# Seven pieces of an embedding table by plain loads and GpSimd adds, in a fused patch-embedding, attention and routed-expert kernel

## The chip, the cores and the metric

The kernel runs on one core of one Trainium2 chip. The metric is the device time of one execution in microseconds, given as the median of several runs. A program runs on five engines, each with its own instruction queue: TensorE (PE in the profile; its weight loads are PEld), VectorE (DVE), ScalarE (ACT), GpSimd (POOL) and SyncE (SP). They are ordered by semaphores alone. DMAs that SP and ACT issue are called hardware_dynamic in the profile, those that POOL issues software_dynamic.

## The reference

Eight images of 3x96x96 are cut into 36 patches each, projected to 192 features and joined with 128 text rows, so there are 8 batches of 164 rows. Then come one attention layer with 12 heads and one routed-expert layer with 16 experts. The part that matters here is one term of the attention: the mean row of a table of 50257x192 numbers.

```
xn = _layernorm(x, ln_w)
avg_wte = jnp.mean(wte, axis=0)                       # 50257 x 192 -> 192
Q = xn[:, None, :, :] * W_qk[None, :, None, :]
attn = jnp.einsum('bhse,bhte->bhst', Q, Q) / math.sqrt(eb)
attn = softmax(where(causal, attn, -inf))
Vv = xn[:, None, :, :] - avg_wte[None, None, None, :]
out = jnp.einsum('bhst,bhte->bhse', attn, Vv) * N_reg # N_reg = 1 / (1..164)
out = out.transpose(0, 2, 1, 3).reshape(xb, sb, H * eb) @ W_o.T
h = h + out
...
h = h + moe(_layernorm(h))   # rms norm, softmax router, 16 experts, 64 rows per expert and batch
```

## The kernel before

**Stages.** After the loads and the patch projection (to about 21 us) there is an attention loop over eight batches, b = 0 to 7 (to about 270 us), then the router and the placing of the rows into a DRAM buffer `xd` ("dispatched" in the profile) with one 112-row block per expert or more, and from about 310 us a loop over these blocks. The rows of `xd` that no token fills have to hold zeros and a marker. Seven DMAs write them from the tile `zeros` ("dispatched<-zeros"), and the scatters into `xd` wait for them on `zero_done`.

**The table.** The table is 38.6 MB and is summed while the attention runs. It is seen as 28 pieces of 128 x 2688 numbers (1344 KB each: 14 rows of the table per partition) and a small tail. The tile `wbuf` has two halves. SP loads pieces 0 and 1 into them (`wte_first`). POOL then issues 26 DMAs that add their piece to what the half holds (`add_wte`, L369 to L377; "wbuf<-in_wte"). The halves take turns, so that two such DMAs are under way, and `add_wte` first waits until the one before it into the same half has landed. Iteration b of POOL's loop issues four of them, k = 0 to 3. At the end DVE sums `wbuf` over its 28 rows (`wte_sum`, four instructions at L700), adds the tail and signals `acc_ready`. The mean is then projected by TensorE near 245 us. It is subtracted late and not in the loop.

**One iteration of attention.** The scores of a batch are made in five rounds: rounds 0 to 2 cover the first 128 rows, four heads each, into the banks `bS`; rounds 3 and 4 cover the last 36 rows. For each round TensorE writes the scores (`score`), DVE takes the row maximum (L663, L667), ACT the exponential with its row sum (L496, L501), DVE the factor `rn` (L673, L675), and POOL multiplies (`normalise`, L387: tile PA for rounds 0 to 2, PB for 3 and 4). TensorE transposes the result (L1062 and on), ACT and DVE split the transposed tile into a high and a low part (L509, L680), and TensorE multiplies it by the values. POOL also makes the left operand of the scores: `weigh` (L365) multiplies the transposed input `zT` by the weights of each head, into AwA (six instructions of 96 x 512 a batch) and AwB (two of 96 x 432).

**Order on POOL.** Iteration b of POOL does, in this order: rounds 3 and 4 of batch b; `add_wte` k = 0; four AwA of batch b + 1; k = 1; two AwA; round 0 of batch b + 1; k = 2; round 1; two AwB; k = 3; round 2. TensorE's first score round of batch b + 1 waits for the first two AwA, so it waits for what stands ahead of them on POOL.

**DVE between two batches.** DVE makes the low parts of the values (`value_low`, L690 and L692), the normalised input of the batch after (`z`, L655 and L657: from SBUF to SBUF), then the row maximum of round 2.

**SP's queue.** SP issues the loads, waits for `zero_ready`, issues the seven zero fills, then the load of `mat32` (tile `pay`), waits for `acc_ready` and loads the first expert weights into the tiles `wx`, which are free until then.

## Time and profile before

| what | value |
|---|---|
| median of 3 runs | 407.25 us (407.04 to 409.11) |
| the profiled execution: its own time | 410.09 us |
| the profiled execution: its span | 408.2 us |
| its granted TensorE clock, mean | 0.942 |
| TensorE busy | 349.9 us, 86% |
| VectorE busy | 196.3 us, 48% |
| GpSimd busy | 181.7 us, 45% |
| ScalarE busy | 119.5 us, 29% |
| moved by DMA | 74.28 MB, mean 182 GB/s |

Busy is the time in which instructions of an engine run. The share is that of the whole span. Times given as a point, such as "at 156.34", are microseconds from the start of the span. In a row of a timeline the first number is the start, the second the length, and what stands in brackets at the end is how long the engine sat idle before it and what released it.

### The profile page before, as it was taken

To read this page: it belongs to the slowest core of one execution; us is meant where nothing else is said; L and a number is where in the kernel's file an instruction comes from. 1 tells how busy PE (TensorE), PEld (TensorE's weight loads), DVE (VectorE), ACT (ScalarE), POOL (GpSimd) and SP (SyncE) were. 2 spreads that over 40 slices of the span, in tenths; PEclk is the share of its full clock that TensorE was granted. 3 is DMA by queue.
4 is the path that set the end of the run, shared out by engine and by line. 5 is a ranking of instruction groups with operands and counts; after the bars stand their busy time and mean duration, and the time that the engine had idled before them with its cause. 6 is when DMAs were issued, how large, how long until landed. Compare 5 with 4: busy or idle time off the path is not lost.

```text
span 408.2 us, 6960 instructions
## 1 busy us (share of the span) xinstructions
PE 349.9 (86%) x2371; PEld 314.5 (77%) x2371; DVE 196.3 (48%) x532; ACT 119.5 (29%) x411; POOL 181.7 (45%) x189
## 2 busy tenths in 40 slices
PE   7878889589789899898899999995684998999990
PEld 3456579578689789797899898895534998999990
DVE  0495865737536456355472575678660221222220
ACT  1115333332744456345543133333100011111110
POOL 3164573385576674857655131611377421111110
PEclk9989999699999999999999999998586898999996
DMA  6599999999999999999995008800133497899700
GB/s 218 193 372 265 233 251 247 256 217 209 200 173 209 212 209 210 205 210 205 207 209 119 0 2 247 217 0 2 53 117 82 137 295 198 267 287 285 240 14 9
DMA packets 20735, 74.28 MB, mean 182 GB/s; under 512 B 3180, under 2 KB 8813, under 8 KB 20202
## 3 DMA queue, kind: packets, MB, share of 16 engines
q0 software_dynamic: 8976, 38.83, 46.3%
q1 hardware_dynamic: 10826, 34.57, 27.4%
q10 hardware_dynamic: 912, 0.62, 0.6%
q8 instruction: 12, 0.20, 0.2%
q14 instruction: 9, 0.07, 0.1%
HBM read 66.12 MB, written 9.25 MB: 185 GB/s over the span
## 4 chain that ended last, share of the span: by engine, by line
DMA 43%; PE 34%; issue 8%; POOL 6%; DVE 3%; SPq 1%; ACT 1%; POOLq 1%; ACTq 1%; DVEq 0%
DMA wbuf<-in_wte 34%; PE bO L991 11%; PE bE L991 10%; PE bJ L991 6%; DMA AwA<-dispatched 6%; PE bS L991 4%; DMA hB<-in_txtB 3%; POOL AwA L365 2%; POOL dispatched L430 2%; POOL wbuf L376 1%; PE bT L1308 1%; POOL PB L387 1%; PE bT L1062 1%; DMA dispatched<-pay,posI 1%; DVE wsum L700 1%
## 5 line engine op out<-in xcount | busy, mean ns | idle before, releaser
L496 ACT ACTIVATE PA<-bS,negmax 128x128 f32<-128x128 f32 x96 | 33.9, 366 | 94.2 <-DVE negmax L663 94.2
L365 POOL TENSOR_TENSOR AwA<-zT,w 96x512 f32<-96x512 f32 x45 | 52.4, 1448 | 7.4 <-ACT zT L478 7.4
L991 PE MATMUL bJ<-wo_sb,oTA 128*128 128x192 f32 x288 | 51.5, 327 | 0.7 <-DVE H L706 0.7
L376 POOL DMA_DIRECT2D wbuf<-in_wte x26 | 32.1, 1255 | 44.3 <-DMA wbuf<-in_wte 43.1
L991 PE MATMUL bO<-PA,wx 96*128 96x112 f32 x384 | 48.0, 284 | 0.5 <-DVE PA L966 0.5
L991 PEld LDWEIGHTS bO<-PA,wx 96*128 96x128 f32 x384 | 47.7, 201 | 0.9 <-DVE PA L966 0.9
L991 PEld LDWEIGHTS bS<-zT,AwA 96*128 96x128 f32 x384 | 46.7, 192 | 1.4 <-issue 0.2
L991 PEld LDWEIGHTS bJ<-wo_sb,oTA 128*128 128x128 f32 x288 | 46.3, 190 | 1.0 <-DVE H L706 0.9
L991 PE MATMUL bS<-zT,AwA 96*128 96x128 f32 x384 | 46.8, 275 | 0.0
L435 POOL DMA_INDIRECT out<-PA,yrow x16 | 15.1, 942 | 64.1 <-DVE PA L980 64.1
L387 POOL TENSOR_TENSOR PA<-PA,rn 128x512 f32<-128x512 f32 x24 | 28.3, 1177 | 24.5 <-DVE rn L675 23.7
L587 ACT ACTIVATE AwA<-bO 128x448 f32<-128x448 f32 x16 | 8.7, 543 | 95.1 <-PE bO L991 95.1
L991 PE MATMUL bE<-wx,AwA 128*112 128x192 f32 x192 | 36.3, 342 | 0.0
L991 PEld LDWEIGHTS bE<-wx,AwA 128*112 128x112 f32 x192 | 32.6, 188 | 0.1
L663 DVE TENSOR_REDUCE negmax<-bS 128x4 f32<-128x512 f32 x24 | 16.4, 684 | 21.1 <-PE bS L991 21.1
L973 DVE TENSOR_SCALAR AwA<-bO 128x224 f32<-128x224 f32 x16 | 6.3, 392 | 39.3 <-PE bO L991 39.3
L387 POOL TENSOR_TENSOR PB<-PB,rn 108x328 f32<-108x328 f32 x16 | 11.7, 732 | 21.6 <-DVE rn L675 21.3
L991 PE MATMUL bS<-zT,AwB 96*108 96x164 f32 x128 | 20.3, 302 | 0.0
L496 ACT ACTIVATION_READ_ACCUMULATOR PA<-bS,negmax 128x1 f32 x96 | 19.6, 204 | 0.0
L514 ACT ACTIVATE oTA<-bO,lncol 128x512 f32<-128x512 f32 x24 | 16.5, 688 | 10.4 <-PE bO L991 9.8
L680 DVE TENSOR_TENSOR PTAL<-bT,PTAH 128x512 fp32r<-128x512 f32 x24 | 15.8, 686 | 7.0 <-ACT PTAH L509 6.9
L980 DVE SCALAR_TENSOR_TENSOR PA<-bE,AwA 112x192 f32<-112x192 f32 x16 | 6.7, 418 | 25.5 <-PE bE L991 25.5
(243 smaller groups left out, 697.1 us busy)
## 6 DMA issues: line engine op xcount, KB each, us to landing
wbuf<-in_wte POOLq DMA_DIRECT2D x26, 1344.0 KB, 12.8
wx<-in_wi SPq DMA_DIRECT2D x16, 576.0 KB, 5.1
wx<-in_wo SPq DMA_DIRECT2D x16, 576.0 KB, 6.4
dispatched<-zeros SPq DMA_DIRECT2D x7, 675.5 KB, 26.5
AwA<-dispatched SPq DMA_DIRECT2D x17, 168.9 KB, 5.9
wbuf<-in_wte SPq DMA_DIRECT2D x2, 1344.0 KB, 11.3
wo_sb<-in_wo_attn SPq DMA_DIRECT2D x1, 1728.0 KB, 6.6
pay<-in_cst SPq DMA_DIRECT2D x1, 1024.0 KB, 39.7
```

Of the source, the lines that this page charges most:

```text
L365: nc.gpsimd.tensor_tensor(o, zT[:, k, ss].unsqueeze(1).to_broadcast(list(o.shape)), w2[:, k, hs].unsqueeze(2).to_broadcast(list(o.shape)), ...
L376: pool.dma_start(wchunk[s], wv[:, ds(c, 1), :].rearrange("p c x -> p (c x)"), accum_op=ALU.add, max_dma_last_dim=WR * EMB * 4 // 2).then_i ...
L387: nc.gpsimd.tensor_tensor(t, t, q.unsqueeze(2).to_broadcast(list(t.shape)), ALU.mult).then_inc(p_ready, 1)
L430: nc.gpsimd.indirect_dma_start(out=xd[:, :], out_offset=bass.IndirectOffsetOnAxis(ap=posI[0:n, j:j + 1], axis=0), in_=pay[0:n, j, :], in_o ...
L435: nc.gpsimd.indirect_dma_start(out=out[:, :], out_offset=bass.IndirectOffsetOnAxis(ap=idx, axis=0), in_=rows, in_offset=None, bounds_check ...
L496: last = nc.scalar.activation(PA[:, h, :], bank[:, j * SA:(j + 1) * SA], ACT.Exp, bias=negmax[:, h:h + 1], accum_out=lsum[:, h:h + 1])
L514: nc.scalar.activation(dst, src, ACT.Copy, scale=lncol[:, 0:1]).then_inc(o_used, 1)
L587: nc.scalar.activation(hT[:, 0:4, :], bO[0][:, 0:4 * T].rearrange("p (c n) -> p c n", c=4), ACT.Relu).then_inc(h0_ready, 1)
L663: nc.vector.tensor_reduce(negmax[:, 4 * r:4 * r + 4], bS[r % 2][:, :].rearrange("p (h s) -> p h s", h=4), X, ALU.max, negate=True).then_in ...
L680: nc.vector.tensor_tensor(dst, src, pt_round(q, 0, bT[0])[0], ALU.subtract).then_inc(tl_used, 1)
L980: nc.vector.scalar_tensor_tensor(ysb[p], bE[0:T, 0:EMB], xb[q][:, D_RP:D_RP + 1], xb[q][:, D_BASE:D_BASE + EMB], ALU.mult, ALU.add).then_i ...
L991: return nc.tensor.matmul(o, l, r, start=start, stop=stop, skip_group_check=True)
```

## The change

Pieces 21 to 27 of the table are no longer added by an accumulating DMA. SP loads them plainly: piece 21 into `plain_acc` (the tile wx0) and pieces 22 to 27, one after the other, into `plain` (wx1). In each of POOL's iterations 0 to 5 GpSimd adds `plain` to `plain_acc` in four instructions of 128 x 672: one at the end of step k = 2 and three at the end of step k = 3. It then waits for its own four adds. SP issues the next plain load after them. POOL's iterations issue three accumulating DMAs, k = 0 to 2, in place of four (two in iteration 5), and the loop runs over pairs of iterations. DVE adds `plain_acc` to the first half of `wbuf` before it sums. On SP, `mat32` and the plain loads stand ahead of the zero fill, so the zero fill is issued after the last plain load.

```diff
+WPLAIN = 7
...
+        plain_acc, plain = wx[0][:, :], wx[1][:, :]
...
+            def plain_loads(sp):
+
+                sp.dma_start(plain_acc, wv[:, WCHUNKS - WPLAIN, :]).then_inc(plain_in, 16)
+                for n in range(1, WPLAIN):
+                    if n > 1:
+                        sp.wait_ge(plain_used, 4 * (n - 1))
+                    sp.dma_start(plain, wv[:, WCHUNKS - WPLAIN + n, :]).then_inc(plain_in, 16)
...
+            sp.dma_start(mat32, cst2_d[:, C_MAT:NCST2]).then_inc(mat_in, 16)
+            plain_loads(sp)
+
             sp.wait_ge(zero_ready, 1)
             for n in range(XROWS // (ZB * T)):
                 sp.dma_start(xd[n * ZB * T:(n + 1) * ZB * T, :].rearrange("(p n) e -> p n e", n=ZB),
                              zeros[0:T, :].unsqueeze(1).to_broadcast([T, ZB, DW])).then_inc(zero_done, 16)
-            sp.dma_start(mat32, cst2_d[:, C_MAT:NCST2]).then_inc(mat_in, 16)
...
+            def add_wte_nth(i, r):
+
+                add_wte(6 * i + r + WBUF, r % 2, 3 * i + r // 2)
+
+            def add_plain(b, p):
+
+                pool.wait_ge(plain_in, 16 * (b + 2))
+                q = slice(p * WR * EMB // 4, (p + 1) * WR * EMB // 4)
+                nc.gpsimd.tensor_tensor(plain_acc[:, q], plain_acc[:, q], plain[:, q], ALU.add).then_inc(plain_used, 1)
+                if p == 3:
+                    pool.wait_ge(plain_used, 4 * (b + 1))
...
-            def iteration(b, more):
+            def iteration(b, i, r, n):
+
+                more = r is not None
                 normalise(b, range(3, SPR))
                 for k in range(4):
-                    if more:
-                        add_wte(4 * b + 4 + k, k % 2, 2 * b + 1 + k // 2)
+                    if k < n:
+                        add_wte_nth(i, r + k)
...
                     elif k == 2:
                         normalise(b + 1, (1,))
                         weigh(b + 1, t_before(b, "z") + 1, (0, 1), (3,))
+                        if more:
+                            add_plain(b, 0)
                     else:
                         normalise(b + 1, (2,))
-
-            with pool.Fori(0, NBATCH - 2) as b:
-                iteration(b, True)
-            iteration(NBATCH - 2, False)
+                        if more:
+                            for p in range(1, 4):
+                                add_plain(b, p)
+
+            with pool.Fori(0, 2) as i:
+                iteration(2 * i, i, 2, 3)
+                iteration(2 * i + 1, i, 5, 3)
+            iteration(4, 2, 2, 3)
+            iteration(5, 2, 5, 2)
+            iteration(NBATCH - 2, 0, None, 0)
...
             def wte_sum(k):
 
+                if k == 0:
+                    dve.wait_ge(plain_used, 4 * (WPLAIN - 1))
                 for s in range(WBUF):
-                    dve.wait_ge(wte_in[s], 16 * (WCHUNKS // WBUF - 1))
+                    dve.wait_ge(wte_in[s], 16 * ((WCHUNKS - WPLAIN - s + 1) // WBUF - 1))
+                if k == 0:
+                    link(nc.vector.tensor_tensor(wbuf[:, 0:WR * EMB], wbuf[:, 0:WR * EMB], plain_acc, ALU.add))
```

The second half of an iteration on POOL (GpSimd) in program order, before: round 1 of `normalise`, the two AwB, the fourth accumulating DMA, round 2, the end of the loop.

```order
L387 TENSOR_TENSOR PA<-PA,rn 128x512
L365 TENSOR_TENSOR AwB<-zT,w 96x432 x2
L376 ISA
L376 DMA wbuf<-in_wte 128x2x1344
L381 REGISTER_ALU
L387 TENSOR_TENSOR PA<-PA,rn 128x512
L413 REGISTER_ALU
L413 COMPARE_AND_BRANCH
```

The same place on POOL after the change, where line numbers are larger (L412 is `normalise`, L378 `weigh`, L400 the new add, L389 the accumulating DMA), and on into the next iteration:

```order
L412 TENSOR_TENSOR PA<-PA,rn 128x512
L378 TENSOR_TENSOR AwB<-zT,w 96x432 x2
L398 ISA
L400 TENSOR_TENSOR wx<-wx 128x672
L406 REGISTER_ALU
L412 TENSOR_TENSOR PA<-PA,rn 128x512
L400 TENSOR_TENSOR wx<-wx 128x672 x3
L402 REGISTER_ALU
L406 REGISTER_ALU
L412 TENSOR_TENSOR PB<-PB,rn 108x328
```

One add now stands behind the two AwB, and three stand between round 2 and rounds 3 and 4 (PB). The DMA between AwB and round 2 is gone.

On DVE (VectorE), in the iteration of batch 6, where the table is summed (L736 is the new add, L738 the sum, L697 and L744 the row maximum and the residual), before:

```order
L680 TENSOR_TENSOR PTAL<-bT,PTAH 128x512
L685 TENSOR_SCALAR oTA<-bE,lncol 128x256 x2
L700 TENSOR_REDUCE wsum<-wbuf 128x48 x2
L663 TENSOR_REDUCE negmax<-bS 128x4
L706 TENSOR_TENSOR H<-bJ,H 96x192
```

and after:

```order
L714 TENSOR_TENSOR PTAL<-bT,PTAH 128x512
L719 TENSOR_SCALAR oTA<-bE,lncol 128x256 x2
L736 TENSOR_TENSOR wbuf<-wbuf,wx 128x2688
L738 TENSOR_REDUCE wsum<-wbuf 128x48 x2
L697 TENSOR_REDUCE negmax<-bS 128x4
L744 TENSOR_TENSOR H<-bJ,H 96x192
```

The new add of 128 x 2688 stands ahead of the two sums, and so ahead of the row maximum of batch 7.

On SP (SyncE), the start of its queue, after the change (L286 is the tail of the table, L288 `mat32`, L268 and L272 the plain loads, L293 the zero fill, L299 and L300 the expert weights):

```order
L286 DMA wtail<-in_wte 81x192
L288 DMA pay<-in_cst 128x2048
L268 DMA wx<-in_wte 128x2688
L272 DMA wx<-in_wte 128x2688 x6
L293 DMA dispatched<-zeros 448x1x386 x7
L299 DMA wx<-in_wi 96x1536
L300 DMA wx<-in_wo 128x1152
```

Before, the seven zero fills stood right behind `wtail` and `mat32` behind them.

## Rows read from the trace of the kernel before

**Rows 1.** The page: busy time; chain that ended last, by engine and line.

```profile
PE 349.9 (86%) x2371; PEld 314.5 (77%) x2371; DVE 196.3 (48%) x532; ACT 119.5 (29%) x411; POOL 181.7 (45%) x189
...
DMA 43%; PE 34%; issue 8%; POOL 6%; DVE 3%; SPq 1%; ACT 1%; POOLq 1%; ACTq 1%; DVEq 0%
DMA wbuf<-in_wte 34%; PE bO L991 11%; PE bE L991 10%; PE bJ L991 6%; DMA AwA<-dispatched 6%; PE bS L991 4%; DMA hB<-in_txtB 3%; POOL AwA L365 2%; POOL dispatched L430 2%; POOL wbuf L376 1%; PE bT L1308 1%; POOL PB L387 1%; PE bT L1062 1%; DMA dispatched<-pay,posI 1%; DVE wsum L700 1%
```

**Rows 2.** Timeline of GpSimd: start, length, instruction, idle before and releaser.

```profile
81.61 1.21 POOL L376 DMA_DIRECT2D wbuf<-in_wte  x1 [1.52 <-DMA wbuf<-in_wte]
...
156.34 1.21 POOL L376 DMA_DIRECT2D wbuf<-in_wte  x1 [2.62 <-DMA wbuf<-in_wte]
157.10 1.52 POOL L387 TENSOR_TENSOR PA<-PA,rn 128x512 f32<-128x512 f32 x1
160.64 0.73 POOL L387 TENSOR_TENSOR PB<-PB,rn 108x328 f32<-108x328 f32 x1 [2.02 <-DVE rn L675]
...
162.80 1.21 POOL L376 DMA_DIRECT2D wbuf<-in_wte  x1 [0.41 <-issue]
163.57 4.48 POOL L365 TENSOR_TENSOR AwA<-zT,w 96x512 f32<-96x512 f32 x4
169.29 1.21 POOL L376 DMA_DIRECT2D wbuf<-in_wte  x1 [1.23 <-DMA wbuf<-in_wte]
170.04 2.52 POOL L365 TENSOR_TENSOR AwA<-zT,w 96x512 f32<-96x512 f32 x2
```

**Rows 3.** The DMAs of 130 to 200 us: issue, count, size, median to landing.

```profile
wbuf<-in_wte POOLq DMA_DIRECT2D x11, 1344.0 KB, 12.5
```

**Rows 4.** Timeline of TensorE at the hand-over between batches.

```profile
76.33 0.42 PE L1023 MATMUL bT<-cst,zA 128*96 128x128 f32 x1 [4.24 <-DVE PTAL L680]
...
101.93 1.04 PE L1062 MATMUL bT<-cst,PA 128*128 128x128 f32 x8
...
114.20 0.39 PE L991 MATMUL bS<-maskA,idb 128*128 128x512 bf16 x1 [0.89 <-POOL AwA L365]
...
156.13 1.04 PE L1062 MATMUL bT<-cst,PA 128*128 128x128 f32 x8
...
166.21 0.39 PE L991 MATMUL bS<-maskA,idb 128*128 128x512 bf16 x1 [1.08 <-POOL AwA L365]
```

**Rows 5.** Stretches: busy PE, PEld, DVE, ACT, POOL; then PE clock, DMA, GB/s.

```profile
68.00:85.00 17.00, 11.56 (x66) 10.33 (x64) 12.06 (x17) 5.94 (x18) 8.30 (x10) 0.80 1.05 252
...
140.00:166.00 26.00, 24.27 (x174) 23.01 (x174) 13.39 (x31) 12.32 (x46) 17.18 (x18) 1.00 1.05 210
```

**Rows 6.** What TensorE waited for, whole span: us, times, longest.

```profile
PE bO L991 <- DVE PTB1L L680: 5.6, 6, 1.5
PE bS L991 <- POOL AwA L365: 5.3, 5, 1.1
```

**Rows 7.** GpSimd's only add of two f32 tiles.

```profile
L422 POOL TENSOR_TENSOR H<-H,cN 128x1344 f32<-128x1344 f32 x1 | 3.1, 3074 | 0.0
```

**Rows 8.** Timeline of VectorE.

```profile
69.39 4.08 DVE L801 TENSOR_REDUCE ws<-wo_sb 128x192 f32<-128x2304 f32 x1
...
100.94 0.38 DVE L655 TENSOR_SCALAR zA<-H,rstd,nmr 128x192 f32 x1 [0.30 <-DVE vBL L692]
...
126.93 0.61 DVE L655 TENSOR_SCALAR zA<-H,rstd,nmr 128x192 f32 x1 [0.30 <-DVE vBL L692]
...
156.51 0.23 DVE L675 TENSOR_SCALAR rn<-rinv,cst 128x4 f32<-128x4 f32 x1
157.40 1.29 DVE L680 TENSOR_TENSOR PTAL<-bT,PTAH 128x512 fp32r<-128x512 f32 x2 [0.41 <-ACT PTAH L509]
...
171.83 0.77 DVE L675 TENSOR_SCALAR rn<-rinv,cst 128x4 f32<-128x4 f32 x1
...
224.71 4.82 DVE L700 TENSOR_REDUCE wsum<-wbuf 128x48 f32<-128x1344 f32 x2
232.16 0.69 DVE L663 TENSOR_REDUCE negmax<-bS 128x4 f32<-128x512 f32 x1 [2.62 <-PE bS L991]
```

More of the change, by code:

```diff
@@ L171, in program @@
         wte_first = sem("wte_first")
+        plain_in, plain_used = sem("plain_in"), sem("plain_used")
         wtail_in, wte_added, dve_step, pool_step = (sem(n) for n in ("wtail_in", "wte_added", "dve_step", "pool_step"))
```

## The prediction

> **What bounds the kernel now.** I read the page first. TensorE is busy 86% of the span, yet the chain that ended last gives 34% to the accumulating DMAs of the table [rows 1]. Taken alone that chain says that the table sets the pace, and that a lighter table would help. So the next view is TensorE itself in one iteration of the loop. From 140 to 166 us it is busy 24.27 of 26 us at a granted clock of 1.00 [rows 5]. There is at most 1.7 us to win in an iteration, whatever the DMAs do.
>
> Then I asked what TensorE waits for in that remainder. In the whole span it waits 5.3 us in five times for the AwA of the first score round, and 5.6 us in six times for PTB1L, a low part that DVE makes [rows 6]. The first is released by POOL. In POOL's timeline [rows 2] the first of the four AwA starts at 163.57, and TensorE's score round starts at 166.21, two AwA later [rows 4]. What stands ahead of it is the DMA issue at 162.80, ahead of that the two PB (from 160.64), and these wait for `rn` from DVE. The DMA at 162.80 did not wait for a landing that the profile shows: 0.41 us of issue. The waits for a landing stand at k = 3 (2.62 us at 156.34) and k = 1 (1.23 us at 169.29). Behind k = 3 comes round 2 at 157.10, and then POOL is idle again for 2.02 us, waiting for DVE; so that wait delays nothing that TensorE asks for. The table and the attention loop run side by side at nearly the same pace, about 6.5 us a piece (156.34, 162.80, 169.29), and the attention loop is the one that the AwA closes.
>
> So the 2.02 us of idle POOL time ahead of the PB, and whatever lies between the PB and the AwA, is the place to watch. The change puts three adds there.
>
> **The change, part by part.**
>
> *Price of an add.* GpSimd adds two f32 tiles once before: 128 x 1344 in 3.07 us [rows 7]. Half of that is 1.54 us for 128 x 672; three are 4.6 us, four 6.1. The AwA are a lower bound by the element: 4.48 us for four of 512 [rows 2], 1.12 each, so 1.47 for 672; three are 4.4. I take 4.6.
> GPSIMD Engine Reference in the Trainium skill, section 3.1, gives 4497 ns for a two-input add of 2048 numbers, twice VectorE's time, and advises against elementwise work there; by it an add would be an estimated 1.48 us and the three 4.4.
>
> *The fourth add, behind the AwB.* It has an idle POOL to itself, but DVE's `z` falls there. At 126.93 zA took 0.61 us, with POOL at work, where it took 0.38 at 100.94 with POOL free; `rn` at 171.83 took 0.77 where 0.23 is normal, and it ended as POOL's pair of AwA from 170.04 did [rows 2, 8]. So these instructions of DVE, from SBUF to SBUF, stand still until POOL's own instruction ends. An add of 1.54 us right behind the AwB should hold up zA or zB, and with them the row maximum of round 2. I put this at 1.6 us; below, it is nothing, if both get in between.
> The Trainium skill, SBUF — State Buffer, section "Who interferes with whom", calls this an exclusive lock for the whole instruction, taken by `tensor_scalar` in its two-port mode; the 0.77 us agrees with it.
>
> *The three adds.* Before, `rn` of round 2 is there at 156.51 + 0.23 = 156.74 [rows 8]. With the 1.6 us it is there at 158.3. Round 2 takes about 1.1 (its 1.52 at 157.10 overlaps a DMA issue), to 159.5. The adds take 4.6, to 164.1. The two PB with the wait for the adds take 1.6, to 165.7. The DMA of k = 0 takes 0.41 and 0.77 (162.80 to 163.57), to 166.9. Two AwA take 2.64 (163.57 to 166.21), to 169.5. Before, it was 166.21: **3.3 us later in each such iteration**. Without the hold on `z` it is 1.7. DVE may also be held at `rn` of rounds 3 and 4, which now fall into the adds; I count nothing more for it, since POOL has to finish the adds anyway.
> This counts in full at the ends of iterations 2, 3 and 4: 9.9 us.
> At the end of iteration 1 the hand-over from the transposes at 101.93 to the score at 114.20 takes 12.3 us in place of 10.1 (156.13 to 166.21) [rows 4], so 2.2 of the 3.3 lie beside what fills it: 1.1 us.
> At the end of iteration 0 DVE is late by its sums over `wo_sb` (4.08 us at 69.39 [rows 8], and TensorE waits 4.24 at 76.33 [rows 4]); the adds lie beside that. A held `z` would push those sums by up to 2 us, and the DMA wait of 1.52 at 81.61 [rows 2] goes, worth at most the 1.1 that TensorE waits. I take +1.0, between -1.1 and +2.
> At the end of iteration 5 nothing asks for the AwA early: the projection of the packed rows stands ahead on TensorE. Nothing.
>
> *One accumulating DMA less.* POOL saves an issue of 0.75 us at k = 3, already in the above, and k = 1 waits no longer. Its pair of AwA then ends about 1.2 us earlier, at 171.3, before `rn` asks for the port at 171.83, so PTB1L is not late. Of the 5.6 us of waits for PTB1L [rows 6] I take back 3.0; between 0 and 5.6.
> The landing itself (12.5 us with two under way [rows 3]) is hidden behind TensorE's work, so its shortening is worth nothing more.
>
> *The sum on DVE.* The new add of 128 x 2688 has no row. Low parts of 128 x 512 take 1.29 us for two [rows 8], so 2688 numbers take 3.4 us. It stands ahead of the sums at 224.71, and behind them DVE was idle 2.62 us before the row maximum at 232.16. So 0.8 us comes out, 1.0 with a wait for POOL's port. If POOL's AwA held it throughout, 2 us.
>
> *Zero fill and `mat32`.* The fill leaves the first 80 us, where the DMAs are full, for about 195 to 230 us. It is wanted at the scatters after 290 us, and the first expert weights wait for the sum of the table at 245 us. Ahead there is one plain load and the last accumulating DMAs, which DVE wants only at 224.71 plus what was lost. Nothing. If that cover is gone, the fill stands ahead of the weights on SP and each us late there is a us late in the block loop.
>
> The sum is 1.0 + 1.1 + 9.9 - 3.0 + 1.0 = **10.0 us**. It is made against the profiled execution, whose own time is 410.09 us (span 408.2), so 420.1. The median of the runs is 407.25, that is 2.8 less, which gives 417.3; I say **417 us**.
>
> **The rivals.**
>
> *A. The table sets the pace after all (0.17).* Speaking for it: the chain gives it 34% [rows 1]; the 0.41 us ahead of k = 0 could hide a landing; and its DMAs are never idle (share 1.05 [rows 5]). Four pieces of 6.5 us are 26 us, just the iteration. If so, three pieces and a plain one let each iteration fall to TensorE's work: 1.7 us in each of five iterations, 8.5 us, **399 us**. It needs POOL to fit its adds into the 2.02 us and the freed waits. Against: 4.6 us do not fit into 2.02.
>
> *B. The adds fit nearly (0.20).* If `z` gets in between and an add takes 1.35 us, each of three iterations loses 1.1 us, the end of iteration 1 nothing, iteration 0 gains 1.1, and the PTB1L wait gives 3.0 back: 3.3 - 1.1 - 3.0 + 0.8 = 0.0, **407 us**. For it: POOL has 17.18 us of work in 26 [rows 5], and even 5 more leaves room. Against: the order on POOL is fixed, and the three adds stand ahead of PB.
>
> *C. The clock follows (0.18).* Where TensorE waited 4.24 us, matmuls of 128 x 128 behind it took 0.42 us, and in 68 to 85 us its clock was 0.80 in place of 1.00 [rows 4, 5]. Between its two levels, 1.2 and 2.4 GHz, that mean is 6.8 us at the lower one; less the 4.24 us of idling, 2.6 us ran at half pace and lost 1.3 us, or 3.4 if the idling was still at the upper level. I take 2. If each of three longer stalls of 3.3 + 1.1 us does the same, 6 us come on top: **423 us**. For it: the stalls would be as long as that one. Against: a wait in the values for DVE may cut a stall into two short ones.
>
> My forecast holds 0.45.
>
> **How the numbers follow.** B lies about no change: of its 0.20 I give 0.03 to faster, 0.12 to the same, 0.05 to slower. A is faster by far, forecast and C are slower. A measurement of this kernel can tell about 0.5% from no change, 2 us. So faster 0.20, same 0.12, slower 0.68. The range goes from just under B, 406, to 424, a little over C. It leaves out A and the far end of C. The forecast's own range is 412 (with 1.7 in place of 3.3 in three iterations) to 421.
>
> **What would show it.** If I am right, POOL's three adds run from about 2 us after TensorE's transposes to 8 us after them; TensorE's wait for AwA rises from 1.1 to above 3 us in iterations 2 to 4 and the iteration from 26 to about 29.5 us; zA or zB is longer or later than 0.38; the waits of POOL for a landing nearly vanish; the row maximum near 232 us has no idle time before it. It would be wrong if the iterations come in under 26 us (A), if an add takes 1 us, or if TensorE's clock falls to the lower level in the loop (C). If the zero fill delays the last pieces or the weights, a wait for them shows on DVE after 225 us or in the block loop.

## The result, and the profile after

The changed kernel takes 430.48 us (median of 4 runs, 428.85 to 431.68). The kernel before takes 408.18 beside it. The ratio is 1.0539, 95% interval 1.048 to 1.0597. The direction was forecast, the size was not: 22 us in place of 10, and outside the range. Some executions run in a slower state, whatever the kernel; the ratios, with their intervals, leave them out, the medians do not. The profiled execution has a span of 430.0 us at a mean granted clock of 0.908, where before it was 0.942.

The page after: busy time, the granted clock in 40 slices, the chain that ended last, and the groups of the new add, of the accumulating DMA and of `rn`.

```profile
PE 362.6 (84%) x2371; PEld 323.4 (75%) x2371; DVE 218.7 (51%) x533; ACT 118.4 (28%) x411; POOL 212.6 (49%) x206
...
PEclk9989988799989999799699999999566698999996
...
PE 37%; DVE 16%; DMA 14%; POOL 12%; issue 12%; ACT 4%; SPq 1%; ACTq 1%; POOLq 1%; DVEq 0%
...
L400 POOL TENSOR_TENSOR wx<-wx 128x672 f32<-128x672 f32 x24 | 38.4, 1620 | 0.0
...
L389 POOL DMA_DIRECT2D wbuf<-in_wte x19 | 25.5, 1368 | 3.5 <-DMA wbuf<-in_wte 3.5
...
L709 DVE TENSOR_SCALAR rn<-rinv,cst 128x4 f32<-128x4 f32 (+1 forms) x40 | 19.1, 476 | 1.4
```

An add takes 1.62 us (1.54 was taken). POOL waits 3.5 us for landings, in place of 43.1 before. In the chain the DMAs fell from 43% [rows 1] to 14%, and DVE rose from 3% to 16%. The chain did point to the table; taking the table out of it brought no gain, not even without the adds (experiment 1). `rn` now takes 476 ns on average, in place of 334 before, and 0.23 us when nothing holds it. The rise is in rounds 3 and 4 alone (from 243 to 847 ns); in rounds 0 to 2 it fell from 396 to 229.

POOL in the iteration of batch 3, the counterpart of [rows 2]:

```profile
162.07 1.77 POOL L378 TENSOR_TENSOR AwB<-zT,w 96x432 f32<-96x432 f32 x2
163.81 1.65 POOL L400 TENSOR_TENSOR wx<-wx 128x672 f32<-128x672 f32 x1
169.18 1.04 POOL L412 TENSOR_TENSOR PA<-PA,rn 128x512 f32<-128x512 f32 x1 [3.73 <-DVE rn L709]
170.18 4.77 POOL L400 TENSOR_TENSOR wx<-wx 128x672 f32<-128x672 f32 x3
175.18 1.43 POOL L412 TENSOR_TENSOR PB<-PB,rn 108x328 f32<-108x328 f32 x2 [0.23 <-DVE rn L709]
176.54 1.19 POOL L389 DMA_DIRECT2D wbuf<-in_wte  x1
177.32 4.46 POOL L378 TENSOR_TENSOR AwA<-zT,w 96x512 f32<-96x512 f32 x4
```

The three adds fill the place where POOL was idle for 2.02 us, and 2.7 us more. Idle time is left, 3.73 us of it, but ahead of round 2, where the order on POOL has nothing to put.

DVE, the counterpart of [rows 8]: the short instructions of iteration 0, then those around the adds of the iteration of batch 3, then the sum of the table.

```profile
48.98 5.20 DVE L639 TENSOR_TENSOR nwz<-nwz,nmr 128x12 f32<-128x12 f32 x1
54.22 3.21 DVE L640 TENSOR_SCALAR nwz<-nwz 128x12 f32<-128x12 f32 x1
...
162.10 1.88 DVE L724 TENSOR_TENSOR vBL<-zB,vBH 36x128 fp32r<-36x128 f32 x1
163.91 1.62 DVE L726 TENSOR_TENSOR vBL<-zB,vBH 36x64 fp32r<-36x64 f32 x1
165.82 0.38 DVE L689 TENSOR_SCALAR zA<-H,rstd,nmr 128x192 f32 x1 [0.29 <-DVE vBL L726]
...
172.23 1.19 DVE L709 TENSOR_SCALAR rn<-rinv,cst 108x2 f32<-108x2 f32 x1
...
173.51 1.45 DVE L709 TENSOR_SCALAR rn<-rinv,cst 108x2 f32<-108x2 f32 x1
...
243.35 2.97 DVE L736 TENSOR_TENSOR wbuf<-wbuf,wx 128x2688 f32<-128x2688 f32 x1
...
251.15 0.68 DVE L697 TENSOR_REDUCE negmax<-bS 128x4 f32<-128x512 f32 x1
```

An instruction on 36 x 64 numbers takes 1.62 us, while the first add of the iteration runs from 163.81. The two `rn` take 1.19 and 1.45 us inside the three adds. In iteration 0 an instruction on 128 x 12 numbers takes 3.21 us. The one of 5.20 us is as long in the kernel before.

TensorE, the counterpart of [rows 4]; the first row is that of the kernel before, for the second:

```profile
59.39 0.44 PE L991 MATMUL bO<-PTB0H,vAH 128*128 128x432 f32 x1 [0.83 <-DVE PTB1L L680]
...
62.36 0.70 PE L1029 MATMUL bO<-PTB0H,vAH 128*128 128x432 f32 x1 [3.87 <-DVE PTB1L L714]
...
83.52 0.42 PE L1061 MATMUL bT<-cst,zA 128*96 128x128 f32 x1 [6.18 <-DVE PTAL L714]
...
120.42 0.39 PE L1029 MATMUL bS<-maskA,idb 128*128 128x512 bf16 x1 [1.93 <-POOL AwA L378]
...
175.41 0.39 PE L1029 MATMUL bE<-PTAH,vAH 128*128 128x256 f32 x1 [1.92 <-DVE oTA L719]
...
176.46 0.60 PE L1029 MATMUL bO<-PTAH,vAL 128*128 128x512 f32 x1
...
179.93 0.61 PE L1029 MATMUL bS<-maskA,idb 128*128 128x512 bf16 x1 [1.17 <-POOL AwA L378]
180.33 3.37 PE L1029 MATMUL bS<-zT,AwA 96*128 96x128 f32 x16
...
185.82 1.95 PE L1029 MATMUL bS<-zT,AwA 96*128 96x128 f32 x16
```

The stall is cut into two (1.92 and 1.17 us), and behind them the same 16 matmuls take 3.37 us that take 1.95 a little later. The windows, columns as in [rows 5], give the clock:

```profile
150.00:180.00 30.00, 25.70 (x175) 23.61 (x176) 16.91 (x31) 11.87 (x46) 23.05 (x22) 0.94 0.86 194
179.00:210.00 31.00, 27.28 (x174) 25.09 (x174) 17.08 (x32) 11.87 (x46) 22.59 (x22) 0.89 0.80 177
```

POOL is busy 23 of 30 us, in place of 17 of 26. TensorE's granted clock is 0.94 and 0.89 here, so a part of these stretches is at the lower of its levels. It fell before the second of the two waits: the matmul at 176.46 takes 0.60 us, and the same one at 172.87, ahead of the first wait, 0.39.

**Where the 22 us went.** The start of TensorE's first score round of each batch, in both timelines:

| from batch to batch | before us | after us | more | forecast |
|---|---|---|---|---|
| 1 to 2 (iteration 0) | 52.32 to 85.01 | 52.26 to 90.92 | 6.0 | 1.0 |
| 2 to 3 | 85.01 to 114.20 | 90.92 to 120.42 | 0.3 | 1.1 |
| 3 to 4 | 114.20 to 139.99 | 120.42 to 150.76 | 4.6 | 3.3 |
| 4 to 5 | 139.99 to 166.21 | 150.76 to 179.93 | 3.0 | 3.3 |
| 5 to 6 | 166.21 to 192.66 | 179.93 to 210.56 | 4.2 | 3.3 |
| 6 to 7 | 192.66 to 229.95 | 210.56 to 248.60 | 0.7 | 0 |
| 7 to the mean of the table | 229.95 to 245.67 | 248.60 to 264.64 | 0.3 | 1.0 |
| low part PTB1L no longer late, in all of them | | | in the above | -3.0 |
| the block loop, from its first rows to the end | 308.45 to 408.2 | 327.63 to 430.0 | 2.6 | 0 |

### The profile page after: what moved, and what is told of

Read it like the earlier page. It is cut to its first block, busy times and chain, and to the rows that moved or that the text cites. A ratio compares the mean times of both kernels' runs of the same rounds, so it can differ in the third digit from the quotient of the medians.

```text
span 430.0 us, 6938 instructions
## 1 busy us (share of the span) xinstructions
PE 362.6 (84%) x2371; PEld 323.4 (75%) x2371; DVE 218.7 (51%) x533; ACT 118.4 (28%) x411; POOL 212.6 (49%) x206
## 4 chain that ended last, share of the span: by engine, by line
PE 37%; DVE 16%; DMA 14%; POOL 12%; issue 12%; ACT 4%; SPq 1%; ACTq 1%; POOLq 1%; DVEq 0%
PE bO L1029 12%; PE bE L1029 12%; DMA AwA<-dispatched 6%; PE bS L1029 6%; DMA wbuf<-in_wte 5%; POOL wx L400 5%; PE bJ L1029 5%; DMA hB<-in_txtB 3%; ACT PA L530 3%; POOL dispatched L464 2%; DVE negmax L697 1%; POOL wbuf L389 1%; DVE nwz L639 1%; POOL AwB L378 1%; DVE wsum L738 1%
## 5 line engine op out<-in xcount | busy, mean ns | idle before, releaser
L530 ACT ACTIVATE PA<-bS,negmax 128x128 f32<-128x128 f32 x96 | 33.9, 366 | 109.8 <-DVE negmax L697 109.8
L412 POOL TENSOR_TENSOR PA<-PA,rn 128x512 f32<-128x512 f32 x24 | 25.4, 1058 | 68.4 <-DVE rn L709 68.4
L378 POOL TENSOR_TENSOR AwA<-zT,w 96x512 f32<-96x512 f32 x45 | 56.8, 1578 | 3.9 <-ACT zT L512 3.9
L1029 PEld LDWEIGHTS bS<-zT,AwA 96*128 96x128 f32 x384 | 50.5, 205 | 1.6 <-issue 0.3
L1029 PE MATMUL bS<-zT,AwA 96*128 96x128 f32 x384 | 50.3, 288 | 0.0
L1029 PEld LDWEIGHTS bJ<-wo_sb,oTA 128*128 128x128 f32 x288 | 47.3, 194 | 1.4 <-DVE H L744 1.2
L400 POOL TENSOR_TENSOR wx<-wx 128x672 f32<-128x672 f32 x24 | 38.4, 1620 | 0.0
L1029 PE MATMUL bE<-wx,AwA 128*112 128x192 f32 x192 | 37.3, 348 | 0.0
L697 DVE TENSOR_REDUCE negmax<-bS 128x4 f32<-128x512 f32 x24 | 16.5, 686 | 22.1 <-PE bS L1029 22.1
L389 POOL DMA_DIRECT2D wbuf<-in_wte x19 | 25.5, 1368 | 3.5 <-DMA wbuf<-in_wte 3.5
L1029 PE MATMUL bE<-PTAH,vAH 128*128 128x256 f32 x48 | 15.2, 317 | 7.0 <-DVE oTA L719 7.0
L1018 DVE SCALAR_TENSOR_TENSOR PA<-bE,AwA 112x192 f32<-112x192 f32 x16 | 6.7, 418 | 26.3 <-PE bE L1029 26.3
L709 DVE TENSOR_SCALAR rn<-rinv,cst 128x4 f32<-128x4 f32 (+1 forms) x40 | 19.1, 476 | 1.4
```

What stands on the lines that cost most here:

```text
L378: nc.gpsimd.tensor_tensor(o, zT[:, k, ss].unsqueeze(1).to_broadcast(list(o.shape)), w2[:, k, hs].unsqueeze(2).to_broadcast(list(o.shape)), ...
L389: pool.dma_start(wchunk[s], wv[:, ds(c, 1), :].rearrange("p c x -> p (c x)"), accum_op=ALU.add, max_dma_last_dim=WR * EMB * 4 // 2).then_i ...
L400: nc.gpsimd.tensor_tensor(plain_acc[:, q], plain_acc[:, q], plain[:, q], ALU.add).then_inc(plain_used, 1)
L412: nc.gpsimd.tensor_tensor(t, t, q.unsqueeze(2).to_broadcast(list(t.shape)), ALU.mult).then_inc(p_ready, 1)
L530: last = nc.scalar.activation(PA[:, h, :], bank[:, j * SA:(j + 1) * SA], ACT.Exp, bias=negmax[:, h:h + 1], accum_out=lsum[:, h:h + 1])
L697: nc.vector.tensor_reduce(negmax[:, 4 * r:4 * r + 4], bS[r % 2][:, :].rearrange("p (h s) -> p h s", h=4), X, ALU.max, negate=True).then_in ...
```

## The experiments

The runs were made on three chips, in groups of four, four and three. So a ratio to the kernel before on the same chip is what compares them, and stretches of one group. "Period" below is the distance between the transposes of `z` of two batches on TensorE, from the timeline. The kernel before has 34.4 (batch 1 to 2), 30.7, 26.2, 26.3, 26.3, 32.9; the changed one has 41.6, 28.6, 29.2, 29.1, 30.8, 36.2.

**1. No adds.**

```diff
-                nc.gpsimd.tensor_tensor(plain_acc[:, q], plain_acc[:, q], plain[:, q], ALU.add).then_inc(plain_used, 1)
+                pool.sem_inc(plain_used, 1)
```

> The changed kernel with its 24 GpSimd adds left out (a bare semaphore increment stands in the place of each), so pieces 22 to 27 of the table are missing from the sum; loads, waits, DMA counts and the late zero fill are as in the changed kernel. Theory 1 (the adds cost the time, by standing ahead of PB on POOL and by holding VectorE's instructions): 410 to 413 us, so 18 us or more come back; what is left is iteration 0, where VectorE is held 3 us by AwA that before came after a wait for a DMA. Rival 2 (the plain loads and the moved zero fill cost it, by traffic): 427 to 431 us, little comes back. Rival 3 (fewer accumulating DMAs and an early DMA queue without zeros are a gain that the adds ate up): under 404 us.

Measured: 415.82 us, ratio 0.9996 (0.996 to 1.0032); the kernel before takes 416.23 on this chip. The number is outside theory 1's 410 to 413, which were meant beside the 408.18 of the first comparison, a ratio of 1.004 to 1.012. Net of what it gives back elsewhere, the change without its adds costs nothing, so the adds and what they set off are the whole loss, and theory 1 holds with a little more coming back than expected. Rival 3 (under 404, a ratio under 0.99) fails too: the lighter table alone is no gain. Inside, the periods are 39.7, 26.7, 26.3, 25.2, 25.3, 31.1. Against the first trace of the kernel before, that is a gain of 4.0 us at batch 2 to 3 and of about 1 us in most of the later ones, and a loss of 5.3 us in iteration 0. Against its other trace (experiment 5) it is 1.5, about 0.5, and 3.9. No trace of the kernel before is from this chip.

**2 and 3. The first add alone, and the other three alone.** The diff is that of the second kernel; the third has (1, 2, 3) in place of (0,).

```diff
+                if p in (0,):
+                    nc.gpsimd.tensor_tensor(plain_acc[:, q], plain_acc[:, q], plain[:, q], ALU.add).then_inc(plain_used, 1)
+                else:
+                    pool.sem_inc(plain_used, 1)
```

> The changed kernel with only the first of the four adds of an iteration (the one behind the two AwB); the other three are bare increments, so three quarters of pieces 22 to 27 are missing from the sum. Theory 1a (the hold of value_low behind that add delays the row maximum of round 2 by 1.6 us and all that VectorE does after it, PB included): 5 to 9 us over the kernel without adds. Rival 1b (its 1.6 us fall into idle time of POOL and VectorE, and all of the loss comes from the three adds ahead of PB): within 2 us of the kernel without adds.

> The changed kernel with only the last three of the four adds (between round 2 and PB); the first is a bare increment, so a quarter of pieces 22 to 27 is missing. Theory 1 with 1a: 3 x 1.6 us less 2 us of idle time, 1.7 us or more in each of iterations 2 to 4, some 5 to 9 us over the kernel without adds. Rival 1b: 12 us or more over it, nearly the time of the changed kernel.

Measured: the first add alone has four executions from 421.28 to 507.97 us and no ratio; the two lowest, 421.28 and 424.31, are 5.5 and 8.5 us over the kernel without adds. The three alone take 428.02 us, ratio 1.0316 (1.0254 to 1.0378). The profiles are steadier. From the transposes of batch 1 to the first expert weights it is 201.6 us without adds (43.46 to 245.03), 209.2 with the first (42.19 to 251.36) and 212.2 with the three (42.06 to 254.27): 7.6 and 10.6 us. The first add has the 5 to 9 us of theory 1a, and rival 1b fails for it. The three miss the 5 to 9 us that I expected: by the profiles they cost 10.6, by the medians 12.2, the 12 that rival 1b said of them, though the ratio of 1.0316 is not nearly that of the changed kernel. So both places cost, and the three adds cost more than theory 1 gave them. The period of the quiet batches (4 to 5) goes from 25.2 to 26.7 and to 27.6; 1.5 and 2.4 make 3.9, and the changed kernel, with all four, has 29.1 there. So the two effects add up where the clock stays. The lower clock behind a hand-over into batches 3 to 6 (5.7 us from one score round to the next, in place of 4.1) comes once with the three adds alone (118.25 to 123.96), three times in the changed kernel, and never with the first add alone or without adds.

**4. The kernel before, zero fill late.**

```diff
+            sp.dma_start(mat32, cst2_d[:, C_MAT:NCST2]).then_inc(mat_in, 16)
+            sp.wait_ge(p_ready, SPR * 5 + 3)
             sp.wait_ge(zero_ready, 1)
...
-            sp.dma_start(mat32, cst2_d[:, C_MAT:NCST2]).then_inc(mat_in, 16)
```

> The kernel before, with the load of mat32 moved ahead of the zero fill and the zero fill held until POOL has done round 2 of batch 5 (near 184 us), so the early DMA queue is free of it; nothing else changes. Theory (the wait for a landing near 55 us kept POOL's next AwA away from VectorE's short instructions; without it they are held 3 us, as in the changed kernel): 409 to 413 us, slower by less load. Rival (the zero fill slowed the early iterations): 402 to 406 us. Neither: 407 to 409 us.

Measured: 423.17 us against 416.23 on that chip, ratio 1.0154 (1.0074 to 1.0234). Less early load makes it slower, which rules out the rival; the theory's 409 to 413 (a ratio of 1.002 to 1.012 beside 408.18) were too low, though the interval reaches them. The trace points to two causes. It is that of the longest of the four executions (429.13 us), so its sizes are rough. Iteration 0 has a period of 39.2 us, in place of 34.4 and 35.8 in the two traces of the kernel before, and VectorE's short instructions are held as without adds (6.50, 0.97 and 0.91 us where 5.20, 0.17 and 0.17 were). So moving the zero fill looks like enough for the long iteration 0. And batch 6 to 7 has 35.1, in place of 32.9: with four accumulating DMAs in each iteration the late fill, issued from 188.13, meets the last pieces of the table, and DVE waits for the last one before its sum:

```profile
236.96 4.72 DVE L702 TENSOR_REDUCE wsum<-wbuf 128x48 f32<-128x1344 f32 x2 [6.70 <-DMA wbuf<-in_wte]
```

**5. The kernel before, once more.** No edit.

> The kernel before, unchanged, profiled beside the next three so that stretches can be compared on one chip. If the longer block loop seen in the last four profiles (106 to 109 us in place of 99.8) belongs to the chip, it is there here too; if it belongs to the changed loads, it is 100 us here. If the longer iteration 0 (39 to 41 us in place of 34.4) belongs to the chip and not to GpSimd meeting VectorE, it is there here too.

Measured: span 403.7, block loop 98.6 us (305.11 to the end). That alone can't tell the chip from the changed loads, but the next two kernels have the changed loads and ran on this chip too, with a block loop of 100.5 us each. So the long block loops of the first four belong to their chip. Iteration 0 is 35.8 us here, 1.4 more than in the first trace. This one DVE row says why:

```profile
63.44 3.83 DVE L692 TENSOR_TENSOR vBL<-zB,vBH 36x64 fp32r<-36x64 f32 x1
```

In the first trace POOL waited for a landing until 65.16 at this place and the same instruction took 0.21 us; here the landing came 2 us earlier, POOL went on at 63.17, and DVE was held. By the next score round nothing of it was left (52.16 to 84.85 us here, 52.32 to 85.01 in the first trace, 32.69 both times), since POOL's wait of 1.52 us for the landing at 81.61 [rows 2] is gone here.

**6. A guard in iteration 0 of the changed kernel.**

```diff
+                    if k == 1 and is0(b):
+                        pool.wait_ge(max_ready, SPR + 1)
...
-            with pool.Fori(0, 2) as i:
-                iteration(2 * i, i, 2, 3)
-                iteration(2 * i + 1, i, 5, 3)
+            iteration(0, 0, 2, 3)
+            iteration(1, 0, 5, 3)
+            iteration(2, 1, 2, 3)
+            iteration(3, 1, 5, 3)
```

> The changed kernel with its loop of iterations 0 to 3 written out, and in iteration 0 POOL waits for the row maximum of round 0 of batch 1 before it issues the second accumulating DMA and the third pair of AwA; so VectorE's five short instructions before that row maximum meet an idle POOL, as they did before the change. Theory: the AwA held them 3.2 us (one of them took 3.21 where 0.17 is normal), so 2 to 4 us less than the changed kernel, ratio to the kernel before 1.043 to 1.050. Rival: the delay of iteration 0 comes from the hold of value_low alone and the rest is slack: within 1 us of the changed kernel, 1.052 to 1.056.

Measured: ratio 1.0436 (1.0367 to 1.0505), in the theory's range; the interval overlaps that of the changed kernel (1.048 to 1.0597), so the times alone do not separate the two. The profiles do, for iteration 0: it is 37.2 us in place of 41.6, and in place of the 40.4 that the next kernel, without this wait, has on the same chip. The instruction that took 3.21 us takes

```profile
54.34 0.17 DVE L643 TENSOR_SCALAR nwz<-nwz 128x12 f32<-128x12 f32 x1
```

A wait put into POOL takes 3 to 4 us out of iteration 0. The loop was written out in the same edit; that was not tried by itself.

**7. The same adds at other places.**

```diff
                         normalise(b + 1, (0,))
+                        if more:
+                            add_plain(b, 0)
...
                     else:
-                        normalise(b + 1, (2,))
-                        if more:
-                            for p in range(1, 4):
-                                add_plain(b, p)
+                        if more:
+                            pool.wait_ge(z_ready, 2 * (b + 3))
+                            add_plain(b, 1)
+                            add_plain(b, 2)
+                        normalise(b + 1, (2,))
+                        if more:
+                            add_plain(b, 3)
```

> The changed kernel with the same 24 adds at other places of POOL's order: the first behind round 0, the second and third ahead of round 2 but behind a wait for both z instructions, the last behind round 2. Theory (place, not the amount of work, makes the cost: where POOL idles and VectorE does nothing that meets it, an add is nearly free): ratio 1.000 to 1.020. Rival (GpSimd's 38 us of adds cost wherever they stand, through VectorE's held instructions): 1.035 or more.

Measured: 410.89 us, ratio 1.0029 (0.9991 to 1.0067). The same 24 adds, and 5% less. POOL's timeline of this kernel:

```profile
131.66 3.18 POOL L400 TENSOR_TENSOR wx<-wx 128x672 f32<-128x672 f32 x2 [1.11 <-DVE zB L694]
134.95 1.04 POOL L412 TENSOR_TENSOR PA<-PA,rn 128x512 f32<-128x512 f32 x1
135.95 1.61 POOL L400 TENSOR_TENSOR wx<-wx 128x672 f32<-128x672 f32 x1
138.18 1.57 POOL L412 TENSOR_TENSOR PB<-PB,rn 108x328 f32<-108x328 f32 x2 [0.62 <-DVE rn L712]
```

Two adds stand in the 3.7 us of idle time ahead of round 2, after `z`. One is left ahead of PB, and POOL still waits 0.62 us for DVE there. The later periods are 25.7 us, as in the kernel before on that chip (25.7 and 25.8). What remains is iteration 0 with 40.4.

**8. The kernel before, with VectorE's sums over `wo_sb` moved.** They stood behind iteration 0, where the first two lines of the diff take them out; the three points in a line stand for the operands.

```diff
-            nc.vector.tensor_reduce(ws[:, 0, :], ...)
-            nc.vector.tensor_reduce(ws[:, 1, :], ...)
...
                 if not more:
+                    dve.wait_ge(wo_in, 16)
+                    nc.vector.tensor_reduce(ws[:, 0, :], ...)
                     dve.wait_ge(late_in, 64)
                     residual_b(0)
...
                     wte_sum(0)
                     wte_sum(1)
+                    nc.vector.tensor_reduce(ws[:, 1, :], ...)
```

> The kernel before with VectorE's two sums over wo_sb (4.08 and 2.08 us) taken from between batches 0 and 1 and put into idle time of batch 6: one ahead of the first packed residual, one behind the first two sums of the table. Theory: TensorE's wait of 4.24 us at 76.33 and the lower clock behind it come from these sums, so 3 to 6 us come back in iteration 0 and at most 1 is lost in batch 6: ratio 0.985 to 0.994. Rival (the wait has another cause, the chain through POOL and ACT): 0.998 to 1.003.

Measured: 408.66 us, ratio 0.9972 (0.9934 to 1.001), a miss: next to the rival's 0.998 to 1.003 and outside the theory's range. TensorE's wait at the transposes did go, and the next one came. Its TensorE:

```profile
71.97 0.28 PE L1023 MATMUL bT<-cst,zA 128*96 128x128 f32 x1
...
82.81 0.61 PE L991 MATMUL bS<-maskA,idb 128*128 128x512 bf16 x1 [4.72 <-POOL AwA L365]
```

And its POOL at that time:

```profile
79.40 1.21 POOL L376 DMA_DIRECT2D wbuf<-in_wte  x1 [3.83 <-DMA wbuf<-in_wte]
```

The transposes come at 71.97, not 77.64, and then TensorE waits 4.72 us for AwA, because POOL waits 3.83 us for a landing. The period of iteration 0 fell to 29.9 us and that of the next batch rose to 34.5, from 28.2. In the first 80 us the table is right behind DVE as the bound of the kernel before. So a lighter table should be worth something there, once DVE is out of the way.

**9 to 11. The pieces put together.** The ninth kernel is the seventh with the guard of the sixth, and the first DMA of an iteration behind the first two AwA:

```diff
-                    if k < n:
+                    if 0 < k < n:
                         add_wte_nth(i, r + k)
                     if k == 0:
-                        weigh(b + 1, t_before(b, "z") + 1, (0, 1), (0, 1))
+                        weigh(b + 1, t_before(b, "z") + 1, (0, 1), (0,))
+                        if n:
+                            add_wte_nth(i, r)
+                        weigh(b + 1, t_before(b, "z") + 1, (0, 1), (1,))
```

The tenth also moves the longer of the two sums over `wo_sb` into batch 6. The eleventh is the tenth with the DMA back ahead of the AwA.

> The adds in the gaps and the wait in iteration 0 together (loop written out), and in each iteration the first accumulating DMA (k = 0) is issued behind the first two AwA and not ahead of them. Theory: three accumulating DMAs per iteration leave the landing enough slack, so the 1.2 us of issue come off the path to the AwA that TensorE waits for (0.8 to 1.1 us per iteration), and iteration 0 gives back 3 us: ratio to the kernel before 0.980 to 0.993. Rival (the loop has no slack left anywhere, a wait moves to the next engine): 0.997 to 1.005.

> The same as the kernel before in this list, and the longer of VectorE's two sums over wo_sb (4.08 us) moved into the idle time of batch 6. In the kernel before, moving both sums gave nearly nothing because POOL then waited 3.8 us for a landing in iteration 0. Theory: with the lighter table that wait is gone, so here the move pays 3 to 5 us: ratio 0.965 to 0.985. Rival (the early DMA queue is still full): no better than without the move.

> The adds in the gaps, the wait in iteration 0 and the moved sum, but the DMA of k = 0 ahead of the AwA as in both original kernels; tells what of the last gain is the DMA's place. Theory: 3 to 6 us above the kernel with all four edits, ratio 0.975 to 0.992.

| kernel | median us | ratio to the kernel before | periods, batch 1 to 7 |
|---|---|---|---|
| 9 | 406.59 | 0.9942 (0.9897 to 0.9987) | 37.4, 27.2, 26.0, 26.0, 26.1, 31.3 |
| 10 | 403.53 | 0.9887 (0.9827 to 0.9948) | 33.0, 27.0, 26.2, 25.7, 26.1, 31.3 |
| 11 | 403.60 | 0.9895 (0.9805 to 0.9984) | 33.9, 26.8, 26.2, 25.8, 26.2, 31.6 |

The tenth is faster than both kernels, 1.1% below the one before. The ninth and the tenth fall short of their expected ranges, the ninth by little. The eleventh is inside its range of ratios, but it was to be 3 to 6 us above the tenth and is not: the DMA's place pays nothing. The moved sum pays here: iteration 0 goes from 37.4 to 33.0 and the next batch keeps its 27, where in the eighth the next batch lost what iteration 0 had gained. In the whole time it is 3.1 us, with intervals that overlap. TensorE of the tenth shows where the gain of the DMA's place went: in the eleventh it waits 0.86 to 0.89 us for AwA at a hand-over, in the tenth it does not, but it waits 0.56 us for PTB1L in place of 0.26, and in most batches 0.4 us or more ahead of the transposes of `z`. The two short waits at 157.02 and 158.21 are in both kernels.

```profile
157.02 0.38 PE L1039 MATMUL bE<-PTAH,vAH 128*128 128x256 f32 x1 [0.29 <-DVE oTA L728]
158.21 0.47 PE L1039 MATMUL bO<-PTAH,vAH 128*128 128x512 f32 x1 [0.23 <-DVE PTAL L723]
166.50 0.43 PE L1039 MATMUL bO<-PTB0H,vAH 128*128 128x432 f32 x1 [0.56 <-DVE PTB1L L723]
179.62 0.28 PE L1071 MATMUL bT<-cst,zA 128*96 128x128 f32 x1 [0.41 <-DVE PTAL L723]
```

## Why the prediction was right or wrong

**Right: the loop was not held by the table.** I read this from the idle times around the AwA, against the chain of the page. Rival A is dead: without adds and with the light table the ratio is 0.9996, and the quiet batches come to 25.2 us, not to TensorE's 24.3.

**Right: the mechanism of the adds, and its size per batch.** The three were forecast to run from 2 to 8 us after the transposes and to push PB and AwA by 3.3 us. In the one batch with no change of clock (4 to 5) the loss is 3.0 us after what PTB1L gave back (0.8 to 0.26 us), so 3.5. Experiments 2 and 3 split it into 1.5 and 2.4, where the forecast had 1.6 (held DVE) and 1.7 (adds beyond the idle time): the second was too small. That the whole came out at 3.5 beside 3.3 is in part luck. It was `value_low`, and not `z`, that was held: its last instruction waited for the add, and `z` came after. The cost is the same. At the end of iteration 1, where 1.1 us was taken, 0.3 was lost.

**Right: PTB1L, outside iteration 0.** Its waits fell to 0.26 us each; 3.7 us came back, 3.0 were taken. In iteration 0 the wait rose from 0.83 to 3.87.

**Right: the sum on DVE, the zero fill.** The add took 2.97 us (3.4 taken), and there is no idle time left ahead of the row maximum; with 2.62 us idle before, that makes 0.3 lost (1.0 taken), and 0.3 is what batch 7 to the mean lost. The 0.7 us of batch 6 to 7 hold the lower clock behind 210.56. The fill was issued from 206.12 and waited for by nobody. Experiment 4 adds that with four accumulating DMAs in each iteration a late fill is not free.

**Too light: `rn` of rounds 3 and 4.** I saw that DVE could be held there by the three adds and counted nothing, since POOL has to finish them anyway. POOL did wait only 0.23 us more. But `oTA` stands right behind in DVE's queue, and TensorE waited 1.92 us for it at 175.41, where the kernel before has no wait in this batch; behind this wait the clock fell.

**Wrong: the term for iteration 0, 1.0 us in place of 6.0.** This is the step that failed most. I wrote that the adds lie beside DVE's sums and that a held `z` would push those by up to 2 us, less a DMA wait. I took the waits of POOL for landings as waste that hides behind other work. Two of them kept POOL out of DVE's way. Near 54.3 us POOL waited 0.69 us before its second run of AwA, and DVE's short instructions slipped through. After the change the landing was there, POOL went on, and one of them was held for 3.21 us. And until 65.16 POOL waited for a landing while DVE did `value_low` in 0.8 us (63.07 to 63.82); after the change POOL was there at the same time, and it took 4.7 (68.31 to 72.97). A third part lies between the two: behind TensorE's wait of 3.87 us at 62.36 its clock was at the lower level, and the matmuls of the values took 4.8 us (62.36 to 67.19) in place of 2.6 (59.39 to 61.98). At the row maximum of round 2 (66.14 before, 73.59 after) this makes 3.0 us from the held instruction, 2.2 from the clock and 2.2 from `value_low`. It goes into DVE's sums over `wo_sb` and from there to TensorE, whose wait at the transposes grew from 4.24 to 6.18 us; POOL's wait of 1.52 us at 81.61 went, and 6.0 is left. The guard shows the first two together (4.4 us of iteration 0), which is why it gave back more than the 3.2 us of the hold. The repeated kernel before shows the hold of `value_low` by chance of a landing, though there it cost nothing by the next score round. The kernel without adds has a long iteration 0 as well (39.7 in place of 41.6), and so has the kernel before with nothing but the zero fill moved (39.2). So some 2 us of it may be the adds', and the rest is not.

**Wrong: the clock, rival C, at 0.18.** It came true at three of the hand-overs. After the score round that follows the stall, the next one starts 5.7 us later (120.42 to 126.15, 179.93 to 185.60, 210.56 to 216.27), and 4.1 where the clock stayed (150.76 to 154.84). That is 1.6 us each, 4.9 us in all, against the 6 of the rival. A stall of 1.9 us was enough each time (at 175.41, 206.19 and 120.42); I had thought that a cut stall speaks against it. I had C as a rival beside the sum, at 2 us a stall, and not as a part of it, and I had it for the three long stalls only, not for iteration 0, where it takes another 2.2 us. The result needed C and a dear iteration 0 together: 10.0 + 5.0 + 4.9 is 20 us, and 2.6 of the block loop bring it to 22.5, 0.7 more than the two spans differ by; the terms that came out smaller are the difference. No run was made to try the clock by itself; its share is read from these rows.

**Open: the block loop.** It is 2.6 us longer after the change. On the chip of experiments 5 to 8 it is 98.6 and 101.0 us in the fifth and the eighth, which have the loads of the kernel before, and 100.5 in the other two. So it may be nothing but that; no run settles it.

## What to carry to other kernels

A wait for a DMA on GpSimd may be what keeps its instructions apart from VectorE's (3 to 4 us here, by the guard), so before a load is taken off its queue, look at what GpSimd will do in the time that comes free and which VectorE instructions stand there. How much idle time an engine has says little; an added instruction costs by what stands right behind it in its queue, and here the same 24 adds cost 5% at one set of places and 0.3% at another. When one wait of TensorE is removed and nothing is gained, as in experiment 8, the next bound may be just the one that the other edit relieves: try them together before either is given up.

## What the hardware did that I had not expected

**VectorE can be held for a whole run of GpSimd instructions, or only for one.** Where the run follows a DMA issue without a break, VectorE gets in only at its end: 5.20 us at 48.98 for 12 numbers per partition, behind four AwA, and 3.83 us at 63.44 in experiment 5. Elsewhere it mostly gets in between two instructions: `value_low` at 163.91 took 1.62 us, one add. But not always: in iterations 1 to 5 of the changed kernel the instruction before it, on 36 x 128 numbers, took 1.88 us (as at 162.10), the time of both AwB, and 1.01 us, the time of one, in the kernel without that add behind the AwB (as at 158.37 in experiment 3). The Trainium skill, SBUF — State Buffer, section "Who interferes with whom", says that whichever of the two engines issues first has the ports that they share for the whole instruction, and the other stands still; the single holds agree, and the held runs are longer than any one instruction. What keeps a run together, the DMA issue ahead of it or something else, was not tried by itself.

**Size does not matter to it.** Instructions on 128 x 12 numbers (3.21 us) and on 36 x 64 (1.62) were held at least as long as one on 128 x 128 (1.17 at 68.31), and `rn` of rounds 3 and 4, on two numbers per partition, rose from 243 to 847 ns on average. They are links of VectorE's chain.

**One short stall can be enough to lower TensorE's clock.** Behind a stall of 1.92 us at 175.41 the matmuls slowed from 176.46 on, and behind the next one, of 1.17 us, the 16 matmuls still took 3.37 us in place of 1.95. It was the same behind 1.93 us at 206.19 and behind 1.93 us at 120.42, where the 16 took 2.52; behind 1.89 and 1.92 us, at 146.31 and 150.76, the clock stayed at the upper level. The length of a stall alone does not tell these apart.
